# Flamingo block with routed experts on one core: transposes moved a slot nearer, the projection in quarters with tokens in partitions

## What is computed

```python
ln = layernorm(layernorm(x)) * gamma_lat + beta_lat ; xn = layernorm(ctx) * gamma_media + beta_media
q = ln @ Wq + bq ; k, v = split(concat([xn, ln]) @ Wkv + bkv)        # 8 heads of 128
attn = softmax(q @ k.T / sqrt(128)) @ v                               # 64 queries on 128 keys
x = x + tanh(g_xattn) * (attn @ Wo + bo)
n = layernorm(x) ; p = softmax(n @ Wr + br)                           # 8 experts
y = sum over the 2 largest p:  p_e * (relu(n @ W1[e] + b1[e]) @ W2[e] + b2[e])
out = x + tanh(g_ffn) * y
```

## Time and profile before

| | |
|---|---|
| median of three executions | 954.1 us |
| the profiled execution | 955.86 us |
| its span, first to last instruction | 953.8 us |
| busy: TensorE / VectorE / ScalarE / GpSimd | 808.2 / 601.6 / 514.6 / 491.2 us |
| mean granted TensorE clock | 0.957 of full speed |
| chain that ended last, TensorE's share | 69% |

### The profile page before, as it was taken

How to read it: one execution, slowest core, us unless ns; L and a number is a source line. 1 busy time by engine, 2 the same in 40 slices (tenths; PEclk the granted TensorE clock), 3 DMA queues, 4 the chain that set the end, 5 groups by cost and what they waited for, 6 DMA issues and landing times.

```text
span 953.8 us, 15888 instructions
## 1 busy us (share of the span) xinstructions
PE 808.2 (85%) x4481; PEld 605.4 (63%) x4481; DVE 601.6 (63%) x1908; ACT 514.6 (54%) x1655; POOL 491.2 (52%) x510
## 2 busy tenths in 40 slices
PE   4747888788999898999899999899999898777760
PEld 4534556464878674878686778677777764656650
DVE  3515475755767756878767677959686754655461
ACT  3537657475757375757475757566666553323320
POOL 2103235252636355766363676657675656572645
PEclk9979999999999999999999999999999999879995
DMA  4953233102121112232212132313131213344532
GB/s 129 372 167 144 86 130 117 50 29 56 53 78 58 52 40 78 64 95 70 74 50 73 51 95 73 89 45 106 51 90 58 81 51 94 96 126 128 139 113 63
DMA packets 113976, 86.14 MB, mean 90 GB/s; under 512 B 11985, under 2 KB 104418, under 8 KB 113890
## 3 DMA queue, kind: packets, MB, share of 16 engines
q1 hardware_dynamic: 99618, 49.32, 18.8%
q0 software_dynamic: 8192, 16.79, 6.0%
q10 hardware_dynamic: 6080, 19.02, 5.0%
HBM read 39.74 MB, written 45.35 MB: 89 GB/s over the span
## 4 chain that ended last, share of the span: by engine, by line
PE 69%; DVE 10%; ACT 7%; issue 5%; SPq 4%; DMA 2%; POOL 2%; POOLq 0%; ACTq 0%; DVEq 0%
PE shared L1072 12%; PE batch L1041 12%; PE batch L1024 9%; PE y_ps L1013 8%; PE hid_ps L1004 8%; PE batch L1032 4%; ACT probs L592 3%; PE shared L947 3%; PE shared L945 3%; PE shared L946 3%; PE xt_ps L988 2%; ACT pT_sb L600 2%; DVE hs L906 2%; SPq L385 2%; PE batch L1004 2%
## 5 line engine op out<-in xcount | busy, mean ns | idle before, releaser
L537 POOL TENSOR_TENSOR probs<-probs,rsums 128x512 f32<-128x512 f32 x128 | 134.6, 1051 | 291.1 <-DVE rsums L900 289.9
L612 ACT ACTIVATE oT<-batch 128x512 f32<-128x512 f32 x128 | 76.5, 598 | 209.0 <-PE shared L1072 114.5
L592 ACT ACTIVATE probs<-batch,neg_max 128x128 f32<-128x128 f32 x512 | 180.4, 374 | 11.8 <-DVE neg_max L894 11.8
L894 DVE TENSOR_REDUCE neg_max<-batch 128x4 f32<-128x512 f32 x128 | 88.0, 687 | 118.8 <-PE batch L1024 117.5
L1041 PE MATMUL batch<-pT_sb,kvn 128*128 128x512 f32 x256 | 140.5, 631 | 24.3 <-ACT pT_sb L600 24.0
L495 POOL DMA_INDIRECT yg<-sorted_y,home x128 | 126.3, 987 | 64.8 <-issue 32.6
L1024 PE MATMUL batch<-kvT,qT 128*128 128x128 f32 x1024 | 141.7, 282 | 17.4 <-ACT oT L612 17.4
L1024 PEld LDWEIGHTS batch<-kvT,qT 128*128 128x128 f32 x1024 | 129.2, 193 | 41.9 <-ACT oT L612 28.7
L482 POOL DMA_INDIRECT sorted_x<-xn,row_of x128 | 130.6, 1020 | 32.5 <-issue 32.0
L1013 PEld LDWEIGHTS y_ps<-wt,hs 128*128 128x128 f32 x848 | 110.1, 196 | 19.1 <-issue 16.3
L1013 PE MATMUL y_ps<-wt,hs 128*128 128x128 f32 x848 | 116.3, 281 | 5.9 <-DVE y_sb L934 5.9
(11 more groups left out here) (132 smaller groups left out, 1226.4 us busy)
## 6 DMA issues: line engine op xcount, KB each, us to landing
sorted_x<-yg ACTq DMA_DIRECT2D x36, 512.0 KB, 3.6
xt<-sorted_x SPq DMA_DIRECT2D x106, 128.0 KB
sorted_y<-y_sb SPq DMA_DIRECT2D x106, 128.0 KB
kv<-in_ctx_dram SPq DMA_DIRECT2D x16, 256.0 KB, 3.8
kv<-in_x_dram SPq DMA_DIRECT2D x16, 256.0 KB, 4.3
xres<-in_x_dram SPq DMA_DIRECT2D x16, 256.0 KB, 3.0
out_dram<-x SPq DMA_DIRECT2D x16, 256.0 KB
sorted_x<-xn,row_of POOLq DMA_INDIRECT x128, 2.3
```

What stands on the lines that cost most here:

```text
L537: nc.gpsimd.tensor_tensor(pv, pv, rsums[:, m % 2, :].unsqueeze(2).broadcast_to([P, 4, P]), ALU.mult).then_inc(probs_ready, 1)
L592: last = nc.scalar.activation(probs[:, m % 2, c * P:(c + 1) * P], batch_ps[m % 3][:, c * P:(c + 1) * P], ACT.Exp, bias=neg_max[:, m % 2, c ...
```

## The change

A batch's transposes go to the end of slot n+1 (`TURN` 1), after everything else but place "c", and its product to the begin of slot n+2 (`OUT` 2), straight after the scores. ScalarE copies `oT` right after exp and `pT_sb` after place "b". The projection becomes four `project` entries a group: heads' `oT` for 128 tokens is stationary and `M` moves, so the result has tokens in partitions; `residual` and `yT` go. VectorE reads a quarter with one operation (times tanh(g), plus `xres`), and GpSimd has before added the bias row `bo_rows` to `xres`, half a group at a time; `bo_rows` is made once. The quarters stand in slots 4, 6, 0 and 2. Everything after them comes one slot sooner (statistics in slots 1 and 2, rows normalised in 3, logits 5, ranking 6, placement and list of tiles 0, table kept 1, scatters 2 to 5, gathers in 0, 1, 6, 7), tiles start a slot sooner and no slot is left out. The diff, its lines of context left out, and without hunks that only change a slot number or drop a declaration:

```diff
@@ -51,7 +51,7 @@
-EXP, TURN = 1, 2
+EXP, TURN, OUT = 1, 1, 2
@@ -61,17 +61,15 @@
-TAIL = B + TURN + 1
+TAIL = B + OUT + 1
 def tile_slots():
-        n = max(n, GB * (LAST_GROUP[k] + 2) + 7 + AHEAD)
+        n = max(n, GB * (LAST_GROUP[k] + 2) + 6 + AHEAD)
-            while n < B + GB and n % GB == 2:
-                n += 1
@@ -90,7 +88,7 @@
-            if n % GB in (0, 1, 2, 7) or n > GB * (G + 1) + 6:
+            if n % GB in (0, 1, 6, 7) or n > GB * (G + 1) + 5:
@@ -103,13 +101,14 @@
-    0: [("turn_kv", 1, 0, "a"), ("place", -2, 0, "b")],
-    1: [("turn_kv", 1, 1, "a"), ("table", -2, 0, "c")],
-    2: [("project", -1, 0, "ab")],
-    3: [("residual", -1, 0, "a"), ("query", 1, 0, "b"), ("query", 1, 1, "c")],
-    4: [("query", 1, 2, "a"), ("query", 1, 3, "b"), ("query", 1, 4, "c")],
-    5: [("turn_x", -1, 0, "a"), ("query", 1, 5, "b"), ("query", 1, 6, "c")],
-    6: [("router", -1, 0, "a"), ("query", 1, 7, "b")],
+    0: [("project", -1, 2, "a"), ("table", -2, 0, "c")],
+    1: [("turn_kv", 1, 0, "a"), ("turn_kv", 1, 1, "b")],
+    2: [("project", -1, 3, "a")],
+    3: [("query", 1, 0, "a"), ("query", 1, 1, "b"), ("query", 1, 2, "c")],
+    4: [("project", 0, 0, "a"), ("turn_x", -1, 0, "b")],
+    5: [("router", -1, 0, "a"), ("query", 1, 3, "b"), ("query", 1, 4, "c")],
+    6: [("project", 0, 1, "a"), ("query", 1, 5, "b")],
+    7: [("query", 1, 6, "a"), ("query", 1, 7, "b"), ("place", -1, 0, "c")],
@@ -173,8 +171,10 @@
+        bo_rows = sb("bo_rows", [P, D])
-        ones_sq = yT[:, 0:P]
+        ones_sq = xT[:, 0:P]
+        tg_bo_sq = xT[:, P:2 * P]
@@ -424,11 +425,13 @@
-                g = n // GB
-                if s == 5 and 0 <= g < G:
-                    at = slice(g * GB, (g + 1) * GB)
-                    wait_shared(sp, shared_out, "residual", g - 1, 0)
-                    sp.dma_start(xres[:, :, :], x[at, :, :].rearrange("(c b) s d -> (b s) c d", b=2)).then_inc(got_xres, 16)
+                for half in range(2):
+                    g = (n + 1 - 4 * half) // GB
+                    if s == (7, 3)[half] and 0 <= g < G:
+                        at = slice(g * GB + 4 * half, g * GB + 4 * half + 4)
+                        wait_shared(sp, shared_out, "project", g - 1, 2 * half + 1)
+                        sp.dma_start(xres[:, 2 * half:2 * half + 2, :],
+                                     x[at, :, :].rearrange("(c b) s d -> (b s) c d", b=2)).then_inc(got_xres[half], 16)
@@ -518,16 +521,25 @@
-                if s == 4 and 0 <= g < G:
+                if s == 3 and 0 <= g < G:
-                g = (n - 3) // GB - 2
-                if 3 <= s <= 6 and 0 <= g < G:
-                    scatter_rows(g, s - 3)
+                for half in range(2):
+                    g = n // GB
+                    if s == (1, 5)[half] and 0 <= g < G:
+                        if g == 0:
+                            pool.wait_ge(bias_ready, 4)
+                        pool.wait_ge(got_xres[half], 16 * (g + 1))
+                        mine = xres[:, 2 * half:2 * half + 2, :]
+                        nc.gpsimd.tensor_tensor(mine, mine, bo_rows[:, :].unsqueeze(1).broadcast_to([P, 2, D]),
+                                                ALU.add).then_inc(xres_ready[half], 1)
+                g = n // GB - 2
+                if 2 <= s <= 5 and 0 <= g < G:
+                    scatter_rows(g, s - 2)
@@ -593,24 +605,20 @@
-                m = n - TURN
+                m = n - OUT
-                    act.wait_ge(pT_ready, m + 1)
-                    wait(act, o_ready, m)
-                    nc.scalar.activation(pT_sb[:, :], batch_ps[m % 3][:, :], ACT.Copy).then_inc(pT_done, 1)
+                    act.wait_ge(o_ready, m + 1)
+                    g, b = m // GB, m % GB
+                    if b % 2 == 0:
+                        wait_shared(act, shared_full, "project", g - 1, b // 2)
+                    nc.scalar.activation(oT[:, :, b * L:(b + 1) * L], batch_ps[m % 3][:, :].rearrange("p (h i) -> p h i", h=H),
+                                         ACT.Copy).then_inc(o_out, 1)
-                if s == 7 and 0 <= g < G:
+                if s == 6 and 0 <= g < G:
-                if 0 <= m < B:
-                    act.wait_ge(o_ready, m + 1)
-                    if m % GB == 0:
-                        wait_shared(act, shared_full, "project", m // GB - 1, 0)
-                    b = m % GB
-                    nc.scalar.activation(oT[:, :, b * L:(b + 1) * L], batch_ps[m % 3][:, :].rearrange("p (h i) -> p h i", h=H),
-                                         ACT.Copy).then_inc(o_out, 1)
@@ -618,6 +626,11 @@
+                m = n - TURN
+                if 0 <= m < B:
+                    act.wait_ge(pT_ready, m + 1)
+                    wait(act, o_ready, m)
+                    nc.scalar.activation(pT_sb[:, :], batch_ps[m % 3][:, :], ACT.Copy).then_inc(pT_done, 1)
@@ -686,6 +693,10 @@
+                    dve.wait_ge(bias_ready, 2)
+                    nc.vector.tensor_copy(tg_bo_sq[:, :], tg_bo[:, :].broadcast_to([P, P])).then_inc(bias_ready, 1)
+                    dve.wait_ge(bias_folded, 2)
+                    nc.vector.tensor_copy(bo_rows[:, :], y_ps[:, P:2 * P]).then_inc(bias_ready, 1)
             def normalise_kv(n, k):
@@ -715,12 +726,13 @@
             def measure_rows(n, s):
-                if s == 3 and 0 <= g < G:
-                    wait_shared(dve, shared_out, "residual", g, 0)
-                    for c in range(4):
+                if s in (1, 2) and 0 <= g < G:
+                    for c in ((0, 1, 2), (3,))[s - 1]:
+                        wait_shared(dve, shared_out, "project", g, c)
-                    dve.wait_ge(stats1_done, g + 1)
+                if s == 2 and 0 <= g < G:
+                    dve.wait_ge(stats1_done, 2 * (g + 1))
@@ -908,11 +920,11 @@
-                    if what == "residual":
-                        wait_shared(dve, shared_full, "residual", g, 0)
-                        dve.wait_ge(got_xres, 16 * (g + 1))
-                        nc.vector.tensor_tensor(x1[:, g, :, :], shared[bank][:, :].rearrange("p (c d) -> p c d", c=4),
-                                                xres[:, :, :], ALU.add).then_inc(shared_out[bank], 1)
+                    if what == "project":
+                        wait_shared(dve, shared_full, "project", g, number)
+                        dve.wait_ge(xres_ready[number // 2], g + 1)
+                        nc.vector.scalar_tensor_tensor(out=x1[:, g, number, :], in0=shared[bank][:, 0:D], scalar=tg[:, 0:1],
+                                                       in1=xres[:, number, :], op0=ALU.mult, op1=ALU.add).then_inc(shared_out[bank], 1)
@@ -980,6 +992,8 @@
+                    pe.wait_ge(bias_ready, 3)
+                    nc.tensor.matmul(y_ps[:, P:2 * P], tg_bo_sq[:, :], ident[:, :], start=True, stop=True).then_inc(bias_folded, 1)
             def turn_tile(i):
@@ -1025,25 +1039,25 @@
+                m = n - OUT
+                if 0 <= m < B:
+                    pe.wait_ge(pT_done, m + 1)
+                    g, b = m // GB, m % GB
+                    nc.tensor.matmul(batch_ps[m % 3][:, :], kvn[:, g % 3, b, :], pT_sb[:, :], start=True, stop=True).then_inc(o_ready, 1)
+                if n in TILE_AT:
+                    hidden_tile(TILE_AT[n])
+                use_shared(n, "a")
+                if n + 1 in TILE_AT:
+                    turn_tile(TILE_AT[n + 1])
+                use_shared(n, "b")
+                if n - 1 in TILE_AT:
+                    output_tile(TILE_AT[n - 1])
-                if n in TILE_AT:
-                    hidden_tile(TILE_AT[n])
-                use_shared(n, "a")
-                m = n - TURN
-                if 0 <= m < B:
-                    pe.wait_ge(pT_done, m + 1)
-                    g, b = m // GB, m % GB
-                    nc.tensor.matmul(batch_ps[m % 3][:, :], kvn[:, g % 3, b, :], pT_sb[:, :], start=True, stop=True).then_inc(o_ready, 1)
-                if n + 1 in TILE_AT:
-                    turn_tile(TILE_AT[n + 1])
-                use_shared(n, "b")
-                if n - 1 in TILE_AT:
-                    output_tile(TILE_AT[n - 1])
             def use_shared(n, place):
@@ -1065,15 +1079,10 @@
                     elif what == "project":
-                        if place == places[0]:
-                            pe.wait_ge(o_out, GB * (g + 1))
-                        each = H // len(places)
-                        for h in range(places.index(place) * each, (places.index(place) + 1) * each):
-                            last = nc.tensor.matmul(sh[:, :], M[:, h, :], oT[:, h, :], start=(h == 0), stop=(h == H - 1))
-                    elif what == "residual":
-                        wait_shared(pe, shared_out, "project", g, 0)
-                        for c in range(4):
-                            last = nc.tensor.transpose(sh[:, c * P:(c + 1) * P], yT[:, c * P:(c + 1) * P], ident[:, :])
+                        pe.wait_ge(o_out, GB * g + 2 * number + 2)
```

(11 more changed lines are left out.)

16 lines of the change are left out of this document (8 added, 8 removed).

## The result

The changed kernel takes **989.4 us** (median of 4 runs, 987.5 to 991.7), beside 954.4 us for the kernel before in the same set: a ratio of 1.037, 95% interval 1.034 to 1.040. The forecast was 976 us with a range of 922 to 1005. The direction was right; the loss is 35 us, where 22 were forecast. The profiled execution took 987.5 us (span 985.8), 0.2% under the median.

The account below looks back on a forecast made before the run. TensorE, busy 85% of the span, was taken as the bound. +30 us before slot 128 and -9 in the tail made +21; 22 was taken, so 954.1 + 22 = 976 us, range 922 to 1005.

Parts of the forecast that it names:

- (c): Slot 3: transposes wait for GpSimd's multiplication, which stands behind the rows' rstd and two scatters; 17 us.
- Rival 1: VectorE isn't late, so only the table and short chains stall, 35 us instead of 102: 908 us; chance 0.17.
- rival 2: VectorE late only at tables and, by half, where there is no tile: 934 us, between 925 and 960; chance 0.15.
- Rival 4: The product still waits for ScalarE's copy, so those 24 us stay: 1000 us; chance 0.03.
- the gaps: TensorE's idle time in groups 1 to 15, 45 and 24 us: at most 69 us to win before slot 128.
- (a): Slot 7's transposes wait behind VectorE's load in slot 6: 1.0 us with tiles, 3.7 or 3.2 without; 32 in sum.
- (b): Slot 1's transposes wait behind VectorE's load in slot 0: 0.6 us with tiles, 3.2 or 1.9 without; 20 in sum.
- (d): Table in slot 0: TensorE waits 5.3 us, the second turned kv in slot 1 1.6 more; five tables, 31 us.
- other slots: Slots whose chain, 4.0 us from exp to exp, is longer than TensorE's work: 2 us.
- TensorE's work: Project in quarters, 7.1 us a group where halves and transposes took 7.3: -3 us in all.
- tail: From slot 128 on, tiles start a slot sooner and only one quarter is in the way: -9 us.
- rival 3: The clock falls too, some 19 stalls of 3 us and more costing 1 us each: 995 us; chance 0.10.

Follow-up runs that it names:

- e8_keys_first: The changed kernel with VectorE's kv normalisation ahead of its read of the project's quarter: 968.4 us, ratio 1.014 to the kernel before.
- e2_spread_keys: The changed kernel with one quarter of the kv normalisation from slot 6 and one from slot 0 moved to slot 7: 955.0 us, ratio 1.002.
- e1_quarters_only: The changed kernel with transposes, product and their copies in the order of the kernel before; quarters and earlier stages stay: 938.3 us, ratio 0.986.
- e4_turn_only: The kernel before with only the new order of transposes and product and their copies, its project in two halves: 958.1 us, ratio 1.006.

## Why the prediction was right, and where its sum was off

**The mechanism held.** The transposes' wait is TensorE's largest, over 50 us, in the slots named; the table's wait is 25.5 us (25 to 30 forecast); the product's is 1.3; groups 7 to 15 take 463.9 us (460 forecast). That VectorE's program order is the cause in slots 7 and 1 is now shown and not argued: its load is the same in `e8_keys_first` and `e2_spread_keys`, only the order differs, and 21 and 34 us go. In slot 3 it is GpSimd's order, as (c) had it: 18.7 of the 20 us there stand behind a multiplication that GpSimd reached straight from its own work. Rival 1, that VectorE with 59 to 63% of busy time isn't late, is out, and so is rival 2. Rival 4 is out by the product's 1.3 us.

**The steps**, for groups 1 to 15, waits per place in the trace of after:

| step | forecast | measured |
|---|---|---|
| what goes: the gaps | -69 | -48 |
| (a) transposes ending slot 7 | 32 | 24.0, 14 times |
| (b) ending slot 1 | 20 | 8.7, 6 times |
| (c) ending slot 3 | 17 | 19.9, 14 times |
| (d) table and turned kv | 31 | 22.3 and 6.6 |
| other slots | 2 | 3 |
| TensorE's work, clock with it | -3 | +5 |
| sum | +30 | +42 |
| start; tail | 0; -9 | -5; -5 |

*The first line is the mis-sized term*, "At most these 69 us can be won before slot 128". It was worked out as the time of the groups less an added-up bill of work, so every us that the bill missed was counted as a gap. The windows have TensorE busy for 661.6 of the 710.0 us, where the bill had 232 + 408 = 640: idle were 48 us, and the other 21 were work. The windows, or the waits over the same stretches, would have told; the waits were read for the whole span only.

*The stalls* were forecast 17 us too high, not too low. (a) is 3.0 us where there is no tile, against 3.7. With a tile it is 0.4 and not 1.0: the normalisation took 2.35 us and not 2.7, in slot 6 and in slot 0 alike, and VectorE was through 10.55 us after the start of slot 6, not 11.05. Slot 0 of group 11 shows it; first the read of the quarter, then the keys' rows, then placement begins:

```profile
580.86 0.35 DVE L926 SCALAR_TENSOR_TENSOR x<-shared,tg,xres 128x128 f32<-128x128 f32 x1 [0.91 <-PE shared L1084]
581.13 0.61 DVE L707 SCALAR_TENSOR_TENSOR kv<-kv,mv,gamma 128x128 f32<-128x128 f32 x2
581.77 0.61 DVE L713 SCALAR_TENSOR_TENSOR kvn<-kv,rstd,beta 128x128 f32<-128x128 f32 x2
...
583.48 0.18 DVE L822 TENSOR_TENSOR both<-shared,next_row 128x32 f32<-128x32 f32 x1
```

The read of the quarter is 0.35 us, as taken from the nearest form and not from the bank's share. (b) is nothing with tiles (0.6 forecast) and 1.5 without (3.2), with 0.84 more spent in the same slot in front of the second turned kv, which stands under (d). (c) is 2.6 in groups 2, 3 and 6 (2.4), 0.5 and 0.8 in groups 1 and 15 (2.6), and 0.2 to 1.7 in those with tiles (0.7): there VectorE's slot 2 got slower (last section). (d) came as worked out; the wait in slot 0 of group 12, the operation of VectorE whose result it turns, and PE's rows:

```profile
638.56 0.25 DVE L865 TENSOR_REDUCE found<-hit 128x2 f32<-128x96 f32 x1
...
638.96 0.59 PE L1102 MATMUL shared<-ident,found 128*2 128x128 f32 x2 [4.80 <-DVE gap L866]
639.48 1.87 PE L1038 MATMUL batch<-kvT,qT 128*128 128x128 f32 x7
```

Placement began at 635.45, 7.5 us after the slot's scores at 627.97 (7.6 forecast), and the slot took 11.5 us.

*The clock*, rival 3, came in part and beside the forecast, not instead of it. The same last row shows it: scores at 1.87 us behind the wait. Over the groups the granted clock is 0.95 and 0.98 where it was 0.98 and 0.99, and TensorE is busy 5 us longer though 3 us of work went. That is some 8 us against the rival's 19: stalls of 3 us and more come 10 times in the groups, not 19.

**The tail** won 5 us instead of 9, and the start 5 us instead of nothing. The new order isn't what won the start: group 1 begins at 79.3 us in the changed kernel, at 78.6 in `e1_quarters_only` with the old order, but at 83.2 in `e4_turn_only` with the new one, against 84.2 before. So it comes with the quarters; how stays open.

**In sum** errors of +21, -17, +8, +4 (tail) and -5 (start) make the 11 us between the sum of 21 and the 32 by which the spans differ; the forecast's own range (962 to 992) held the result at its edge. That it did is in part luck: the two largest errors, gaps put 21 us too high and stalls 17 too high, cancel in the sum.

## What to carry to other kernels

A spare slot between two engines is what lets a third be late with little harm; before spending it, write down for every slot when each engine in the chain is through in program order, and don't go by its share of busy time. Two edits that are each harmless can meet on the same slack (-1.4% and +0.6% made +3.7%), so time them apart. And size what a change can win by the waits of the stretch itself, not by its time less a bill of work.

## What the hardware did that wasn't expected

**The cost of two engines side by side moved instead of growing.** By the groups of VectorE (busy us, mean ns), the kernel before

```profile
L696 DVE SCALAR_TENSOR_TENSOR kv<-kv,mv,gamma 128x128 f32<-128x128 f32 x128 | 59.7, 507 | 6.1 <-DMA Wr_f<-in_L_ffn_Wr_dram 4.4 <-POOL rstd L527 1.8
L711 DVE CAST latT_hi<-kvT 128x512 fp32r<-128x512 f32 x16 | 7.0, 438 | 0.0
```

and the changed one

```profile
L707 DVE SCALAR_TENSOR_TENSOR kv<-kv,mv,gamma 128x128 f32<-128x128 f32 x128 | 39.1, 347 | 6.1 <-DMA Wr_f<-in_L_ffn_Wr_dram 4.3 <-POOL rstd L530 1.8
L722 DVE CAST latT_hi<-kvT 128x512 fp32r<-128x512 f32 x16 | 19.0, 1184 | 0.0
```

The keys' normalisation won 21 us of VectorE's time, as it left the company of GpSimd's multiplication, and the cast of the latents lost 12: in slot 2 of group 11 it takes 1.90 us, from 591.50 to 593.40, while GpSimd is at a scatter until 592.02 and multiplies from 592.05 to 593.10; in groups without tiles, where GpSimd does nothing when it starts, it takes 0.41. The Trainium skill, page "SBUF — State Buffer", section "Who interferes with whom", says that VectorE's casts can run in a mode that takes the port pair shared with GpSimd, and that whoever is second is blocked for the whole instruction. The lengths agree with it: the cast ends 0.3 us after the multiplication does. That the cast was second isn't plain from the rows, since it starts 0.55 us ahead of the multiplication, but it does start within the scatter. Yet the 32 additions on GpSimd cost the kernel nothing. That such an overlap counts only where the slowed engine is the late one would explain it and isn't shown.

**The clock added to what a stall costs.** Behind a stall of 1.9 us the next slot took 4.06 us, behind one of 3.0 in the same place 5.69, as the granted clock fell there. It fell behind five of the six stalls of 3.0 us and behind one of the six of 1.9 us. That is part of why moving one operation by a slot was worth 34 us.

**Two chips differ by 5% on one kernel**, 951 and 1002 us, so times of different chips are compared here as ratios to the kernel before on the same chip.
